# Routed tiles of a fused attention and expert layer: rows split to fp16 halves before they are turned, and turned by DMA instead of by TensorE

## The chip, the cores and the metric

The kernel runs on one core of a Trainium2 chip, as one launch. Its engines are TensorE (PE, with its weight loads PEld), VectorE (DVE), ScalarE (ACT), GpSimd (POOL) and SyncE (SP), which only issues DMAs here. The metric is the device time of one execution in microseconds, the median of several runs. Before the change it is 1236.01 us.

## What is computed

The input has 2 sequences of 2048 tokens of 256 numbers in fp32. The first half is a delta-rule attention block with a residual. The second half, which the change touches, is a mixture of experts:

```python
x = x + attn(layernorm(x))                        # q, k, v by projection and causal convolution, chunks of 64
h = layernorm(x)
scores = sigmoid(h @ centroids.T)                 # 8 experts
_, top_idx = top_k(sigmoid(h @ centroids.T + routing_bias), 2)
top_w = softmax(scores at top_idx)
shared = sum over 2 shared experts of gelu(h @ Wfc_sh.T) @ Wproj_sh.T      # 256 -> 1024 -> 256
routed = sum over the 2 chosen experts of top_w * (gelu(h @ Wfc_r.T) @ Wproj_r.T)
out = x + h + shared + routed
```

All of it is to come out at fp32 accuracy. The expert matmuls reach it with fp16 operands: a number is scaled and split into a high fp16 half and a low one (the rest), and a product is made of three passes: high by high, high by low, low by high.

## The kernel before, in words

**Work.** The attention runs first, in groups of 512 tokens. Beside it the first seven 256-row tiles already go through the two shared experts. From about 590 us on only expert work is left, in *units*, each one tile of 256 rows by one expert: 10 units of the five *early* tiles (two shared experts each), 36 *routed* tiles, 8 units of the four *final* tiles. A routed tile holds rows that chose one expert. The rows come from the table `x2n_d` in DRAM through an indirect DMA, and its result rows go back by another one, to `yt_d`. The first four routed tiles are of two half tiles with an expert each.

**A unit.** PE turns the tile (`turn`, line 1449): four transposes of 128 x 128 fp32 into a PSUM bank, so that the model dimension lies on the partitions. ACT makes the fp16 high half of it (`x_high_half`, 1155), DVE the low half (`x_low_half`, 1937); both lie in `xs`, one buffer for even and one for odd tiles. PE's `up` then does 4 x 12 matmuls of 256 columns, ACT the gelu and the high half of its result, DVE the low half (`low`, 1746), PE's `down` 48 more matmuls, and DVE scales the result to `yo` (`y_of`, 1973).

**Order.** `late_units` (236) writes one order for PE, ACT and DVE alike: step k does `up` of unit k+1, `turn` of unit k+2, `down` of unit k. Most of the routed steps are a hardware loop over pairs of tiles (`Fori`), the rest is straight code. The argument `looped` says how far the loop goes: for PE and ACT over all units up to tile 41, for DVE up to tile 33. The engines wait for each other through counting semaphores: `x_turned`, `x_high`, `x_low`, `up_done`, `h_low`, `y_out` and so on.

**Queues.** POOL issues the gathers and the scatters. Per tile i: wait until PE has turned tile i-2 (its buffer `xg` is then free), gather tile i by two DMAs of 128 rows, wait for `y` of tile i-4, scatter that by two DMAs. SP loads the expert weights piece by piece (`load_piece`, 691) into `wstage`, where ACT and DVE split them (`split_high`, `split_low`); the last two of the 32 pieces are needed before the first routed tile. It also stores the sums of the early tiles (`store_acc`), and, when all scatters have landed (line 784), loads `yt_d` for the closing sums.

Of the kernel before, what the change touches and what calls it, by code (L numbers as in the profile page):

```python
# [7 lines left out]
ALU = mybir.AluOpType  # L8
# [84 lines left out]
def pieces_of(k):  # L93

    return range(EP + sum(LOADS[:k]), EP + sum(LOADS[:k + 1]))

# [139 lines left out]
def late_units(eng, turn, up, down, between=None, spare=None, looped=L_TILES):  # L236

    units = [(early_tile(v), e) for v in range(EARLY) for e in range(N_SH)]  # L240
    units += [(routed_tile(i), 0) for i in range(L_TILES)]
    base = N_SH * EARLY

    def step(k):
        if k + 1 < len(units):
            up(*units[k + 1])
        if k + 2 < len(units) and units[k + 2][1] == 0:
            turn(units[k + 2][0])
        down(*units[k])
        if spare and k + 1 < len(LOADS):  # L250
# [69 lines left out]
def build(nc, x, w_proj, conv_w, g_col, w_o, cent, bias, w_ffn,  # L320
          ident, lvl_masks, eye2, head_sel, head_ones, block_tri, row_iota, tile_iota, pref, lane_iota, col_iota, tok_base, part_iota, out):
    ctx = ExitStack()
    with ctx:
# [50 lines left out]
        assert late <= 8192  # L374

# [170 lines left out]
        x_low = sem("x_low")  # L546
        up_done = sem("up_done")
# [68 lines left out]

        def x_there(t):

            if t.routed:
                return x_gathered[t.par], 16 * XB * (t.half - G_ROUTED // 2 - (G_ROUTED % 2) * (1 - t.par) + 1 if t.half is not None  # L620
                                                    else t.i // 2 + 1)
            return x_loaded[t.par], 16 * t.loaded()

# [18 lines left out]
        def _(sp):  # L642
# [26 lines left out]
            def load_base(t):  # L669
# [9 lines left out]
                sp.dma_start(bt[t.par], rows_of(base_d, t.rows)).then_inc(base_in[t.par], 16)  # L679

# [119 lines left out]
        def _(pool):  # L800
# [82 lines left out]
            def tile_looped(k, j):  # L883
                t, done = looped_tile(k, j), looped_tile(k, j - SCATTER_LAG)
                pool.wait_ge(x_turned, t.turn - 1)
# [30 lines left out]
            def load_final(q):  # L916

                t = routed_tile(R_TILES + q)
                pool.wait_ge(x_turned, t.turn - 1)
# [11 lines left out]
        def _(act):  # L931
# [223 lines left out]
            def x_high_half(t):  # L1155
                act.wait_ge(x_turned, t.turn + 1)
# [27 lines left out]
            late_units(act, x_high_half, unit_of, nothing, spare=split)  # L1184
# [3 lines left out]
        def _(pe):  # L1188
# [260 lines left out]
            def turn(t):  # L1449
                pe.wait_ge(*x_there(t))  # L1450
                if not isinstance(t.g, int) or t.turn:

                    pe.wait_ge(x_low, t.turn)
# [16 lines left out]
            def up(t, e):  # L1470
# [8 lines left out]
                pe.wait_ge(x_low, t.turn + 1)  # L1479
# [27 lines left out]
            late_units(pe, turn, up, down, between, spare)  # L1507
# [3 lines left out]
        def _(dve):  # L1511
# [425 lines left out]
            def x_low_half(t):  # L1937
                dve.wait_ge(x_high, t.turn + 1)
# [65 lines left out]
            late_units(dve, x_low_half, unit_of, y_of, between=between, spare=split, looped=R_TILES)  # L2004
# [67 lines left out]
```

## Time and profile before

| | us |
|---|---|
| runs | 1230.71, 1236.26, 1236.01; median 1236.01 |
| the profiled execution's own time | 1232.95 |
| its span | 1231.2 |
| PE busy | 1114.2 (90%) |
| DVE busy | 694.7 (56%) |
| ACT busy | 622.5 (51%) |
| POOL busy | 365.0 (30%) |
| up passes (line 1378), 3072 matmuls | 352.9 |
| down passes (line 1398), 3264 matmuls | 373.2 |

The span is the time from the first to the last instruction in the trace; the execution's own time has the start and the end of the launch with it. Busy time of PE counts the modelled pipeline, so what two groups of matmuls cost is best read from the distance between their starts. The last two rows of the table are the largest groups of instructions: together they are about 60% of the span. Idle time of an engine matters only where another engine waits for it.

### The profile page before, as it was taken

The numbers are of one execution on the slowest core, as the hardware profiler recorded it, in microseconds if no ns is written. First come the engines' busy times: TensorE is split into PE (matmuls) and PEld (weight loads), VectorE is DVE, ScalarE is ACT, GpSimd is POOL, SyncE is SP. The second block draws the span as 40 slices with busy tenths as digits, with TensorE's granted clock in tenths as the row PEclk, the third lists the DMA queues.
The fourth block names the chain that finished last, engine by engine and source line by source line (L and its number), as shares of the span: only waits on it lengthen the run. The fifth ranks groups of instructions, "written<-read, shape, count | busy, mean of one in ns | idle before, by whom it ended". The sixth has DMA issues, their size and how long they took to land.

```text
span 1231.2 us, 25608 instructions
## 1 busy us (share of the span) xinstructions
PE 1114.2 (90%) x9320; PEld 959.5 (78%) x9321; DVE 694.7 (56%) x1211; ACT 622.5 (51%) x1117; POOL 365.0 (30%) x320
## 2 busy tenths in 40 slices
PE   4596889999999998877988989999999999999996
PEld 1464768787878787766877878898999998999996
DVE  4667857676767675575689642333333333333377
ACT  4565556756565655355633643444444444444442
POOL 0415343424252425122011112334334334333100
PEclk9698879999999999998999989999999999999998
DMA  3202020202020102253222421111111111111456
GB/s 131 69 18 69 1 77 1 78 10 78 10 78 10 61 10 95 78 156 112 95 86 78 138 61 57 43 50 52 43 51 49 45 51 47 47 51 51 145 197 230
DMA packets 54088, 86.36 MB, mean 70 GB/s; under 512 B 6656, under 2 KB 39296, under 8 KB 53888
## 3 DMA queue, kind: packets, MB, share of 16 engines
q1 hardware_dynamic: 46336, 64.37, 16.2%
q0 software_dynamic: 7680, 20.98, 5.5%
q8 instruction: 52, 0.85, 0.3%
q14 instruction: 20, 0.16, 0.0%
HBM read 60.16 MB, written 25.17 MB: 69 GB/s over the span
## 4 chain that ended last, share of the span: by engine, by line
PE 65%; DVE 11%; issue 11%; ACT 6%; POOL 5%; DMA 2%; SPq 0%; DVEq 0%; ACTq 0%; POOLq 0%
PE ps L1398 25%; PE ps L1378 22%; PE ps L1232 4%; PE ps L1389 3%; PE ps L1222 2%; PE ps L1297 2%; POOL W L823 2%; PE ps L1456 2%; POOL W L842 2%; PE ps L1304 1%; ACT W L1071 1%; DVE late_room L1749 1%; PE ps L1358 1%; DVE W L1560 1%; DVE W L1652 1%
## 5 line engine op out<-in xcount | busy, mean ns | idle before, releaser
L1378 PE MATMUL ps<-late_room,W 128*128 128x256 f16 x3072 | 352.9, 273 | 28.5 <-DVE late_room L1749 22.6
L1398 PE MATMUL ps<-W,late_room 128*128 (+1 forms) x3264 | 373.2, 274 | 0.3 <-DVE late_room L1749 0.3
L1378 PEld LDWEIGHTS ps<-late_room,W 128*128 (+1 forms) x3072 | 298.6, 98 | 70.4 <-DVE late_room L1749 28.5
L1398 PEld LDWEIGHTS ps<-W,late_room 128*128 128x128 f16 x3264 | 321.7, 99 | 40.4 <-DVE late_room L1749 0.5
L1097 ACT ACTIVATE ps<-ps 128x512 f32<-128x512 f32 x272 | 158.6, 583 | 354.5 <-PE ps L1378 316.8
L1749 DVE SCALAR_TENSOR_TENSOR late_room<-ps,late_room 128x512 f16<-128x512 f32 x272 | 181.0, 687 | 233.4 <-ACT late_room L1102 233.4
L1102 ACT ACTIVATE late_room<-ps 128x512 f16<-128x512 f32 x272 | 155.7, 595 | 2.5
L1560 DVE SCALAR_TENSOR_TENSOR W<-W 128x512 f32<-128x512 f32 x144 | 109.1, 758 | 10.2 <-ACT W L959 6.8
L940 ACT COPY W<-ps 128x512 f32<-128x512 f32 x112 | 61.5, 589 | 86.7 <-PE ps L1297 70.4
L1232 PE MATMUL ps<-W 128*128 128x512 f16 x384 | 97.3, 399 | 7.1 <-DVE W L1575 3.8
L1997 DVE TENSOR_SCALAR late_room<-ps 128x512 f32<-128x512 f32 x36 | 24.9, 691 | 97.7 <-PE ps L1398 97.7
L1232 PEld LDWEIGHTS ps<-W 128*128 128x128 f16 x384 | 38.7, 103 | 49.1 <-issue 10.2
L1297 PE MATMUL ps<-W 128*128 128x128 f32 x320 | 50.3, 307 | 18.3 <-DVE W L1610 11.1
L1297 PEld LDWEIGHTS ps<-W 128*128 128x128 f32 x320 | 45.7, 217 | 23.7 <-DVE W L1610 14.4
L862 POOL DMA_INDIRECT late_room<-x2n_d,gath x52 | 51.4, 988 | 30.9 <-POOL gath L886 21.2
L873 POOL DMA_INDIRECT yt_d<-late_room,scat x52 | 51.1, 983 | 29.2 <-POOL scat L891 21.3
L1206 PE MATMUL ps<-idt,W 128*128 128x128 f32 x256 | 39.8, 302 | 18.7 <-ACT W L1082 12.8
L823 POOL TENSOR_TENSOR W<-W 128x512 f32<-128x512 f32 x40 | 47.2, 1214 | 24.7 <-ACT W L1021 24.7
L1610 DVE TENSOR_TENSOR W<-W,ps 128x512 f32<-128x512 f32 x40 | 27.4, 684 | 46.8 <-PE ps L1304 46.8
L1206 PEld LDWEIGHTS ps<-idt,W 128*128 128x128 f32 x256 | 32.1, 158 | 23.9 <-issue 12.9
L846 POOL TENSOR_TENSOR W<-W 128x4 f32<-128x4 f32 x8 | 9.0, 1120 | 139.4 <-DVE W L1537 139.4
L862 POOL DMA_INDIRECT late_room<-x2n_d,idx x20 | 19.5, 976 | 90.1 <-PE ps L1456 76.4
(188 smaller groups left out, 1372.1 us busy)
## 6 DMA issues: line engine op xcount, KB each, us to landing
wstage<-in_w_ffn SPq DMA_DIRECT2D x40, 512.0 KB, 3.8
W<-yt_d SPq DMA_DIRECT2D x16, 512.0 KB, 5.8
late_room<-in_x SPq DMA_DIRECT2D x8, 512.0 KB, 4.6
W<-in_x SPq DMA_DIRECT2D x8, 512.0 KB, 4.1
x2n_d<-W SPq DMA_DIRECT2D x8, 512.0 KB, 3.1
base_d<-W SPq DMA_DIRECT2D x8, 512.0 KB, 3.6
late_room<-base_d SPq DMA_DIRECT2D x16, 256.0 KB, 4.2
acc_d<-late_room SPq DMA_DIRECT2D x12, 256.0 KB, 2.2
```

The source lines that it names most:

```text
L823: pool.tensor_tensor(CT[:, s - 1], AT, masks[:, s].unsqueeze(1).to_broadcast([P, GT, P]), ALU.mult).then_inc(masked, 1)
L862: pool.indirect_dma_start(out=xg[t.par][:, c], out_offset=None, in_=x2n_d, in_offset=bass.IndirectOffsetOnAxis(ap=rows, axis=0)).then_inc( ...
L940: act.copy(dst, ring.bank(name)).then_inc(ring.empty(n, name)[0], 1)
L1097: act.activation(up_bank(n, c), up_bank(n, c), ACT.Gelu, scale=1.0 / (X_SCALE * W_SCALE)).then_inc(gelu_done, 1)
L1102: act.activation(hs[b][:, 0, 2 * c:2 * c + 2].rearrange("p f t -> p (f t)"), up_bank(n, c), ACT.Copy, scale=H_SCALE).then_inc(h_high, 1)
L1206: by_tile(ring, n, name, lambda to, k: pe.transpose(to, src[:, k, d * P:(d + 1) * P], idt[:]))
L1232: last = pe.matmul(to, wp[:, hw, d, m * P:(m + 1) * P], xnT[:, hx, d], start=(q == 0), stop=(q == len(parts) - 1))
L1297: by_tile(bk, n, f"Y{s}", lambda to, k: pe.matmul(to, CT[:, s - 1, k], X[b][:, k], start=True, stop=True))
L1378: last = pe.matmul(up_bank(n, c)[:, f * XT:(f + 1) * XT], weight(slot, d, hw, cols), x_halves[:, hx, d], start=(q == 0), stop=(q == len(pa ...
L1398: last = pe.matmul(down_bank(b)[:, c * D:(c + 1) * D], hs[b][:, hh, f, c * P:(c + 1) * P], weight(slot, DB + f // 4, hw, cols), start=(q = ...
L1560: dve.scalar_tensor_tensor(conv_at(m, b), pre[:, m, t:t + GRP], cw[:, m, t:t + 1], conv_at(m, b), ALU.mult, ALU.add).then_inc(conv_step, 1)
L1749: dve.scalar_tensor_tensor(lo, up_bank(n, c), H_SCALE, hi, ALU.mult, ALU.subtract).then_inc(h_low, 1)
```

## The change

For the 36 routed tiles the order of splitting and turning is swapped. ACT and DVE now split the gathered rows as they lie in SBUF, into `xh` (new, one buffer for each parity, 128 x 2 x 2 x 256 fp16), and SP turns both halves with two DMA transposes per tile, one for each group of 128 rows, straight into `xs`. PE has no transposes for routed tiles. The split of a tile stands one step earlier in the common order than the turn did: step k splits the rows of unit k+3. The buffer `xg` is free for the next gather when DVE has made the low half (`row_low`), not when PE has turned it. The early and final tiles are turned by PE as before. The loops of PE and ACT now end at tile 31, as DVE's does, and the remaining tiles are straight code.

```diff
+def by_dma(t):
+    return t.routed and not (isinstance(t.g, int) and t.i >= R_TILES)
...
 def late_units(...)
-        if k + 2 < len(units) and units[k + 2][1] == 0:
+        if k + 2 < len(units) and units[k + 2][1] == 0 and not by_dma(units[k + 2][0]):
             turn(units[k + 2][0])
+        if rows and k + 3 < len(units) and units[k + 3][0].routed and by_dma(units[k + 3][0]):
+            rows(units[k + 3][0])
         down(*units[k])
...
             up(looped_tile(k, j + 1), 0)
-            turn(looped_tile(k, j + 2))
+            if rows:
+                rows(looped_tile(k, j + 3))
             down(looped_tile(k, j), 0)
...
+        xh = [sb(f"xh{b}", [P, XB, 2, D], F16) for b in range(2)]
...
 SP:
+            def turn_rows(t):
+                if not isinstance(t.g, int):
+                    settled(sp, up_done, 4 * (t.unit() - 1))
+                else:
+                    sp.wait_ge(up_done, 4 * (t.unit() - (1 if t.i >= 2 else N_SH - t.i * (N_SH - 1))))
+                settled(sp, row_low, t.i + 1)
+                for c in range(XB):
+                    sp.dma_start_transpose(out=xs[t.par].rearrange("p q d t -> p (q d) t")[:, :, c * P:(c + 1) * P],
+                                           in_=xh[t.par][:, c].rearrange("p q d -> p (q d)")).then_inc(rows_turned[t.par], 16)
...
                 for e in range(N_SH):
+                    if e and v + 2 >= EARLY:
+                        turn_rows(routed_tile(v + 2 - EARLY))
                     load_before(N_SH * v + e)
...
+            for i in range(2, PEELED):
+                turn_rows(routed_tile(i))
             for v in range(2):
                 load_base(final_tile(v))
+            pairs = (R_TILES - 2 - PEELED) // 2
+            with sp.Fori(PEELED // 2, PEELED // 2 + pairs) as k:
+                for j in range(2):
+                    turn_rows(looped_tile(k, j))
+            for i in range(PEELED + 2 * pairs, R_TILES):
+                turn_rows(routed_tile(i))
...
 POOL, tile_looped (and alike in gather_static):
-                pool.wait_ge(x_turned, t.turn - 1)
+                pool.wait_ge(row_low, t.i - 1)
...
 ACT:
+            def row_high_half(t):
+                act.wait_ge(*x_there(t))
+                if not isinstance(t.g, int) or t.i >= 2:
+                    act.wait_ge(rows_turned[t.par], 16 * X_TURNS * of_parity(t))
+                act.activation(xh[t.par][:, :, 0], xg[t.par], ACT.Copy, scale=X_SCALE).then_inc(row_high, 1)
...
-            late_units(act, x_high_half, unit_of, nothing, spare=split)
+            late_units(act, x_high_half, unit_of, nothing, spare=split, looped=R_TILES - 2, rows=row_high_half)
...
 PE, up:
-                pe.wait_ge(x_low, t.turn + 1)
+                if by_dma(t):
+                    pe.wait_ge(*turned_rows(t))
+                else:
+                    pe.wait_ge(x_low, turns(t) + 1)
...
-            late_units(pe, turn, up, down, between, spare)
+            late_units(pe, turn, up, down, between, spare, looped=R_TILES - 2)
...
 DVE:
+            def row_low_half(t):
+                dve.wait_ge(row_high, t.i + 1)
+                dve.scalar_tensor_tensor(xh[t.par][:, :, 1], xg[t.par], X_SCALE, xh[t.par][:, :, 0],
+                                         ALU.mult, ALU.subtract).then_inc(row_low, 1)
```

How the instructions stand: first SP's queue around the last weight pieces, before. `wstage` is the landing place of the weights, `acc_d` the store of an early tile's sums, `base_d` the residual rows; the square brackets name the semaphores waited for.

```order
L685 DMA late_room<-x2n_d 128x2x256 [waits x_turned]
L698 DMA wstage<-in_w_ffn 128x1024 [waits rw_low] x4
L679 DMA late_room<-base_d 128x2x256 [waits y_out]
L689 DMA acc_d<-late_room 128x2x256 [waits y_out]
L698 DMA wstage<-in_w_ffn 128x1024 [waits rw_low] x4
L689 DMA acc_d<-late_room 128x2x256 [waits y_out] x2
L679 DMA late_room<-base_d 128x2x256 [waits y_out] x2
```

The same place now (`late_room<-xh` is a tile's rows turned into `xs`, which lies in `late_room`):

```order
L737 DMA wstage<-in_w_ffn 128x1024 [waits rw_low] x2
L717 DMA_TRANSPOSE late_room<-xh 128x4x128 [waits up_done,row_low]
L717 DMA_TRANSPOSE late_room<-xh 128x4x128
L737 DMA wstage<-in_w_ffn 128x1024 [waits rw_low] x2
L728 DMA acc_d<-late_room 128x2x256 [waits y_out]
L717 DMA_TRANSPOSE late_room<-xh 128x4x128 [waits up_done,row_low]
L717 DMA_TRANSPOSE late_room<-xh 128x4x128
L728 DMA acc_d<-late_room 128x2x256 [waits y_out]
L717 DMA_TRANSPOSE late_room<-xh 128x4x128 [waits up_done,row_low]
L717 DMA_TRANSPOSE late_room<-xh 128x4x128
```

The pair of tile 0 stands between the last four weight loads, that of tile 1 between the last two stores, and the others follow. Second, ACT in the loop of the routed tiles, the end of one tile's unit and the start of the next, before (1097 is the gelu, 1102 the high half of its result, 1158 the high half of the turned tile):

```order
L1097 ACTIVATE ps<-ps 128x512 [waits up_done]
L1102 ACTIVATE late_room<-ps 128x512 [waits gelu_done] x2
L1156 REGISTER_ALU
L1158 ACTIVATE late_room<-ps 128x512 [waits up_done,x_turned]
L1096 ISA
L1097 ACTIVATE ps<-ps 128x512 [waits up_done]
```

And now (1152 is the gelu, 1157 its high half, 1220 the high half of the gathered rows):

```order
L1152 ACTIVATE ps<-ps 128x512 [waits up_done]
L1157 ACTIVATE late_room<-ps 128x512 [waits gelu_done] x2
L1217 ISA
L1219 ISA [waits x_gathered1]
L1220 ACTIVATE xh<-late_room 128x2x256 [waits rows_turned1]
L1151 ISA
L1152 ACTIVATE ps<-ps 128x512 [waits up_done]
```

The instruction has kept its place behind the unit's last high halves, but belongs to a tile one further on; it waits for the gathered rows and for the transposes that last read its buffer, where it waited for PE's turn. DVE's list changes in the same way.

## Rows read from the trace of the kernel before

**Rows 1.** The page, parts 1 and 2: engines; busy tenths in 40 slices.

```profile
PE 1114.2 (90%) x9320; PEld 959.5 (78%) x9321; DVE 694.7 (56%) x1211; ACT 622.5 (51%) x1117; POOL 365.0 (30%) x320
...
PE   4596889999999998877988989999999999999996
...
DVE  4667857676767675575689642333333333333377
```

**Rows 2.** Windows: us, busy us (x instructions) by engine, granted clock, DMA share, GB/s.

```profile
900.00:1000.00 100.00, 100.00 (x918) 90.03 (x917) 36.34 (x55) 43.38 (x81) 38.97 (x55) 1.00 0.15 47
...
sum 300.00, PE 300.00 PEld 270.11 DVE 107.64 ACT 131.13 POOL 117.96; mean PE 100.00 PEld 90.04 DVE 35.88 ACT 43.71 POOL 39.32
```

**Rows 3.** Timeline, two beats: start, duration, engine, line, what, [idle before].

```profile
960.08 0.60 PE L1456 MATMUL ps<-idt,late_room 128*128 128x128 f32 x4
...
960.52 5.40 PE L1398 MATMUL ps<-W,late_room 128*128 x48
...
965.76 5.40 PE L1378 MATMUL ps<-late_room,W 128*128 128x256 f16 x48
...
969.12 0.97 POOL L873 DMA_INDIRECT yt_d<-late_room,scat  x1 [0.30 <-issue]
...
971.00 0.60 PE L1456 MATMUL ps<-idt,late_room 128*128 128x128 f32 x4
...
972.65 0.62 ACT L1158 ACTIVATE late_room<-ps 128x512 f16<-128x512 f32 x1
...
973.52 0.68 DVE L1940 SCALAR_TENSOR_TENSOR late_room<-ps,late_room 128x512 f16<-128x512 f32 x1
...
981.91 0.60 PE L1456 MATMUL ps<-idt,late_room 128*128 128x128 f32 x4
```

**Rows 4.** Line L1456, PE's transposes: count, ns min/median/max.

```profile
L1456 PE MATMUL ps<-idt,late_room x196: 272/273/301, 599.1 to 1200.6; 128*128 128x128 f32 x196
```

**Rows 5.** Timeline, the last early tile's steps to the first routed tile.

```profile
707.52 5.40 PE L1378 MATMUL ps<-late_room,W 128*128 128x256 f16 x48
...
709.58 1.46 SPq L698 DMA_DIRECT2D wstage<-in_w_ffn  x2
...
712.76 0.60 PE L1456 MATMUL ps<-idt,late_room 128*128 128x128 f32 x4
...
714.89 2.02 ACT L1137 ACTIVATE W<-wstage 128x1024 f16<-128x1024 f32 x2
...
719.25 2.35 DVE L1917 SCALAR_TENSOR_TENSOR W<-wstage,W 128x1024 f16<-128x1024 f32 x2
...
723.49 0.82 PE L1389 MATMUL ps<-late_room,W 128*128 128x128 f16 x6 [4.88 <-issue]
```

**Rows 6.** Groups by line, 700 to 1231 us: busy us, mean ns, idle before.

```profile
L1940 DVE SCALAR_TENSOR_TENSOR late_room<-ps,late_room 128x512 f16<-128x512 f32 x44 | 30.0, 682 | 0.0
...
L1158 ACT ACTIVATE late_room<-ps 128x512 f16<-128x512 f32 x44 | 27.1, 616 | 0.0
...
L1917 DVE SCALAR_TENSOR_TENSOR W<-wstage,W 128x1024 f16<-128x1024 f32 x5 | 5.9, 1218 | 0.0
...
L1137 ACT ACTIVATE W<-wstage 128x1024 f16<-128x1024 f32 x4 | 4.0, 1073 | 0.0
```

**Rows 7.** Waits of SP's queue, 590 to 1231 us: total, times, longest.

```profile
SPq L784 <- DMA yt_d<-late_room,dst: 404.6, 1, 404.6
```

**Rows 8.** The page, parts 3 and 6: queues; issues, KB each, us to landing.

```profile
q1 hardware_dynamic: 46336, 64.37, 16.2%
...
wstage<-in_w_ffn SPq DMA_DIRECT2D x40, 512.0 KB, 3.8
...
acc_d<-late_room SPq DMA_DIRECT2D x12, 256.0 KB, 2.2
...
late_room<-x2n_d POOLq DMA_DIRECT2D x16, 128.0 KB, 2.4
...
late_room<-x2n_d,gath POOLq DMA_INDIRECT x52, 2.8
```

More of the change, by code:

```diff
@@ L95, in pieces_of, with turns @@
     return range(EP + sum(LOADS[:k]), EP + sum(LOADS[:k + 1]))
+X_TURNS = XB
+TURNED = EARLY
+def by_dma(t):
+    return t.routed and not (isinstance(t.g, int) and t.i >= R_TILES)
+def turns(t):
+    return t.g - G_EARLY if t.g < G_ROUTED else t.g - G_EARLY - R_TILES
 class Ring:
@@ L233, in final_tile, with late_units @@
     return Tile(G_FINAL + v, REST_ROWS[EARLY + v])
-def late_units(eng, turn, up, down, between=None, spare=None, looped=L_TILES):
+def late_units(eng, turn, up, down, between=None, spare=None, looped=L_TILES, rows=None):
     units = [(early_tile(v), e) for v in range(EARLY) for e in range(N_SH)]
@@ L546, in build @@
         x_low = sem("x_low")
+        row_high = sem("row_high")
+        row_low = sem("row_low")
+        rows_turned = [sem(f"rows_turned{b}") for b in range(2)]
         up_done = sem("up_done")
@@ L615, in weight, with of_parity, turned_rows @@
             return W[:, bass.ds(slot + k, 1), half, cols].rearrange("p a n -> p (a n)")
+        def of_parity(t):
+            return t.half - G_ROUTED // 2 if t.half is not None else t.i // 2
         def x_there(t):
             if t.routed:
-                return x_gathered[t.par], 16 * XB * (t.half - G_ROUTED // 2 - (G_ROUTED % 2) * (1 - t.par) + 1 if t.half is not None
-                                                    else t.i // 2 + 1)
+                return x_gathered[t.par], 16 * XB * (of_parity(t) + 1)
             return x_loaded[t.par], 16 * t.loaded()
+        def turned_rows(t):
+            return rows_turned[t.par], 16 * X_TURNS * (of_parity(t) + 1)
         def conv_at(m, b):
@@ L867, in gather_static @@
                 t = routed_tile(i)
-                pool.wait_ge(x_turned, t.turn - 1)
+                if i >= 2:
+                    pool.wait_ge(row_low, i - 1)
+                else:
+                    pool.wait_ge(x_turned, EARLY - 1 + i)
                 for c in range(XB):
@@ L884, in tile_looped @@
                 t, done = looped_tile(k, j), looped_tile(k, j - SCATTER_LAG)
-                pool.wait_ge(x_turned, t.turn - 1)
+                pool.wait_ge(row_low, t.i - 1)
                 pool.tensor_copy(gath[:, j, :], idx[:, bass.ds(t.i * XB, XB)]).then_inc(gath_copied, 1)
@@ L918, in load_final @@
                 t = routed_tile(R_TILES + q)
-                pool.wait_ge(x_turned, t.turn - 1)
+                if q < 2:
+                    pool.wait_ge(row_low, R_TILES - 1 + q)
+                else:
+                    pool.wait_ge(x_turned, EARLY + q - 1)
                 for c in range(XB):
@@ L1155, in x_high_half @@
             def x_high_half(t):
-                act.wait_ge(x_turned, t.turn + 1)
+                act.wait_ge(x_turned, turns(t) + 1)
                 act.wait_ge(up_done, 4 * (t.unit() - (1 if t.routed else N_SH)))
@@ L1450, in turn @@
                 pe.wait_ge(*x_there(t))
-                if not isinstance(t.g, int) or t.turn:
-                    pe.wait_ge(x_low, t.turn)
+                if turns(t):
+                    pe.wait_ge(x_low, turns(t))
                 for d in range(DB):
@@ L1478, in up @@
                     pair_slots[t.i] = slots
-                pe.wait_ge(x_low, t.turn + 1)
+                if by_dma(t):
+                    pe.wait_ge(*turned_rows(t))
+                else:
+                    pe.wait_ge(x_low, turns(t) + 1)
                 for c in range(4):
@@ L1937, in x_low_half @@
             def x_low_half(t):
-                dve.wait_ge(x_high, t.turn + 1)
+                dve.wait_ge(x_high, turns(t) + 1)
                 hi, lo = (xs[t.par][:, q].rearrange("p d t -> p (d t)") for q in range(2))
                 dve.scalar_tensor_tensor(lo, turn_bank, X_SCALE, hi, ALU.mult, ALU.subtract).then_inc(x_low, 1)
+            def row_low_half(t):
+                dve.wait_ge(row_high, t.i + 1)
+                dve.scalar_tensor_tensor(xh[t.par][:, :, 1], xg[t.par], X_SCALE, xh[t.par][:, :, 0],
+                                         ALU.mult, ALU.subtract).then_inc(row_low, 1)
             def unit_of(t, e):
@@ L2002, in between @@
                     router(part)
-            late_units(dve, x_low_half, unit_of, y_of, between=between, spare=split, looped=R_TILES)
+            late_units(dve, x_low_half, unit_of, y_of, between=between, spare=split, looped=R_TILES - 2, rows=row_low_half)
 def constants():
```

## The prediction, made before the changed kernel was run

> **What bounds the kernel now.** I read the page's first two parts first, to see which engine is busy and in which part of the span [rows 1]: PE 90% over all, and 9 in every slice from the 25th to the last but one, where DVE stands at 3. Then the windows of the routed stretch [rows 2]: in 800 to 1100 us PE is busy 300.00 us out of 300, at a granted clock of 1.00 (full speed, the 2.4 GHz level), with DVE at 36%, ACT 44%, POOL 39% and the DMA engines at 0.15. So in this stretch every nanosecond of PE's own work is a nanosecond of the span, and what the other engines do is free as long as it comes in time.
>
> Then the timeline of one beat [rows 3]. The reader is to see the pattern: 4 transposes at 960.08, 48 down matmuls at 960.52, 48 up matmuls at 965.76, 4 transposes at 971.00. A beat is (981.91 - 960.08)/2 = 10.915 us for each routed tile. The transposes take 960.52 - 960.08 = 0.44 us of it (the 0.60 in the row counts the modelled tail of the last one; the start of the next group is what matters), the two matmul groups 5.24 us each: 10.48 us without the transposes, 0.435 us less. In that row pattern the up pass that ends at 971.00 is followed on ACT by the last high halves and the x high half (ends 973.27) and on DVE by the x low half (ends 974.20). All transposes of the kernel, 196, are in one group [rows 4]: 5 early tiles, 36 routed, 8 final, by 4.
>
> **What goes.** PE loses 36 x 4 = 144 transposes and their waits: 36 x 0.435 = 15.7 us. Most of the 36 stand in the full stretch. The first two are worth a look. Tile 0's turn (712.76) is followed by the down pass, DVE's y, two weight splits, and only then PE's restart at 723.49 [rows 5]: this chain hangs on the end of the down pass, so it moves forward by the whole 0.44. I count all 36.
>
> **What is exchanged.** ACT's high half (616 ns from PSUM) and DVE's low half (682 ns from PSUM) [rows 6] are replaced by the same arithmetic on the gathered rows in SBUF, also 128 x 512. The nearest rows are the weight splits from SBUF [rows 6]: 1073/2 = 0.54 us on ACT for 512 elements and 1218/2 = 0.61 us on DVE (two SBUF inputs, as here). So about 0.1 us less for each engine, and with strided halves perhaps 0.1 us more; hidden either way: ACT and DVE are busy 44 and 36 us in 100 [rows 2]. I take zero.
>
> **What is added.** Per tile two DMA transposes on SP, each turning 128 rows of 512 fp16 numbers (128 KB), four 128 x 128 blocks. SP stands still from the last store of the early tiles to 1145 us (its one wait is 404.6 us [rows 7]), so issuing costs nothing there. The time they have: rows of tile i are split behind the up pass of tile i-2, so the low half is ready about 3.2 us after that pass ends (974.20 - 971.00 [rows 3]). PE then does a down, an up and a down pass before it needs tile i: 3 x 5.24 = 15.7 us. That leaves 12.5 us for issue, both transposes and the semaphore. Two limits follow. One is latency: with two buffers, the beat is (3.2 + L + 5.24)/2, below 10.48 while L is below 12.5. The other is rate: a pair must take the queue less than D = 10.48 us.
>
> No transpose by DMA is in the trace, so D is bounded by other rows. Below: 256 KB out of SBUF land 2.2 us after issue, and the 128 KB rows of the final tiles 2.4 us [rows 8]; a pair at plain speed is 3 us. Towards the other end: SP's queue passed 46336 packets in 16.2% of 16 engines' span [rows 8], 0.162 x 1231.2 x 16 / 46336 = 0.069 us per packet on an engine. If a pair is cut into the 256-byte rows of its blocks, that is 2 x 128 x 4 = 1024 pieces, 64 per engine, 4.4 us. In 32-byte pieces it would be 512 per engine, 35 us, and in single 2-byte numbers 8192 per engine, 565 us. The nearest row is the plain transfer of equal size; I take D = 4 to 5 us, which is hidden with 7 us to spare, and keep the rest for the slower rival.
>
> The Trainium skill bears on this twice. *DMA: Bandwidth & Descriptors*, section "Latency and other measured facts", gives DMA transposes 261 GB/s in one kernel; an estimate by it is 1.0 us of moving per pair, less than the rows' lower bound. *VectorE: DVE Perf Modes*, section "The three transpose paths", speaks against the change: 1309 ns by DMA for one 128 x 128 block, 390 ns on TensorE. Eight blocks one after the other would be an estimated 10.5 us, just at the beat without transposes, so even this leaves the sum as it is but no reserve. On PE the trace disagrees with such single-shot figures (0.11 us for each of a run of four [rows 3]), so I give the 1309 ns little weight as a rate.
>
> **Waits added and what queues behind them.** ACT's row split waits for the gathered rows, and behind it stand the gelus of the next unit, for which PE waits. POOL's order per beat is gather, then the scatter of a tile four earlier, which waits for y [rows 3]. The scatter ahead of tile i's gather ends 970.09 - 965.76 = 4.3 us after the down pass that it waits for, and that pass ends 5.24 us behind the up pass of tile i-4: so the gather starts 9.6 us after the end of that up pass; it lands (2.8 us [rows 8]) some 15 us after that end. It is split behind the up pass of tile i-2, at 2 x 10.48 + 1.8 = 22.8 us. Nearly 8 us to spare. The first two gathers wait for turns of early tiles, as before, and are over a beat ahead of their splits. DVE's wait on ACT's half is the one it has now. PE's wait on x_low becomes a wait on the transposes. The split of the buffers xh waits for the transposes of two tiles earlier, over by then.
>
> **The last weight pieces.** SP's queue now has tile 0's pair ahead of the last two weight loads. The pair waits for the low half of tile 0, near 705.5; the loads wait for the splits until 709.58 [rows 5], so the pair's wait holds nothing. Their data does share the engines: if the pair takes over 4 us, the loads (3.8 us to landing [rows 8], ACT's split at 714.89) slip by the excess less about 1 us, and the first routed tile with them. At 4.4 us: nothing.
>
> **Sum.** 36 x 0.435 off, nothing added: -15.7 us. The profiled execution took 1232.95 us (span 1231.2), so 1217.3; the median shown is 1236.01, by which it would be 1220.3. I take 1219, between the two. The likeliest case's own range is 1212 to 1224 (the before runs alone differ by 5.5 us).
>
> **Rivals.**
> *The transposes set the beat (slower).* Place: SP's queue, tiles 2 to 35. From D = 10.48 us the beat is D; at 10.95 us the gain is eaten (34 x 0.46 = 15.7); beyond it each microsecond costs 34. At D = 12: 1219 + 34 x 1.52 = 1271; at 35 us, 1219 + 834 = 2053. For it: no such operation in the trace, small pieces are what a transpose must come down to somewhere, and the engines are shared with gathers and scatters. Against it: the DMA engines are 0.15 busy in the stretch [rows 2], and it needs more than three times a plain transfer's time. Chance 0.25, of which 0.03 for the far ends.
> *At the edge.* D or L close to the limits (D 10.6 to 11.3, or L about 13 since gathers and scatters interleave): 1230 to 1242, no measurable change. For and against as above. Chance 0.10.
> *A late start.* The first pair delays the last weight pieces, or the first splits wait for a gather: D = 8 us gives 8 - 4 = 4 us of slip less 1, so 1222. One-off, still faster. For it: [rows 5] has about a microsecond of slack there. Against it: D would have to be well above 4.4. Chance 0.12.
> *PE does not keep its rate.* The end of the PE loop moves from tile 41 to tile 31, ten tiles more are straight code. A straight pass takes 712.76 - 707.52 = 5.24 us [rows 5], a looped one the same [rows 3], so I give this 0.01 (about 1225).
> The forecast has the rest, 0.52.
>
> **How the numbers follow.** Faster or slower here means by more than 0.5%, 6 us, about what a measurement of this kernel can tell from no change. Faster: 0.52 + 0.12 + 0.01 = 0.65. Same: 0.10. Slower: 0.25. The range: 1211 below, with 0.02 under it; above, it takes in the late start, the edge and the mildest of the slower rival, up to 1246, with 0.18 beyond.
>
> **What would show it.** In the page after: 52 PE transposes in place of 196, and a beat of 10.48 us between starts of down passes at 900 to 1000 us, PE still 100.00 at clock 1.00. DMA_TRANSPOSE issues on SP, 72 of them, with a time to landing under 6 us. PE without a wait on DMA in the routed stretch. Wrong if up matmuls (now L1439) wait for the xs transposes by DMA: then the beat equals what the queue takes per pair. The late-start rival is seen at the first routed tile: PE starting it later than 723. If ACT's split idles on the gather, my count of POOL's order is off.

## The result, and the profile after

| | before | after |
|---|---|---|
| median of 6 runs each, us | 1231.94 (1229.38 to 1236.26) | 1223.01 (1220.9 to 1225.27) |
| the profiled execution's own time | 1232.95 | 1220.9 |
| its span | 1231.2 | 1218.9 |

The ratio is 0.9921, 95% interval 0.9896 to 0.9946: faster by 8.9 us in the medians and by 12.1 us between the two profiled executions, where 15.7 us had been forecast. The time lies in the range and the sign is right. The median of 1236.01 us given above for the kernel before is that of its first three runs; with three more it is 1231.94. The question is where the rest of the 15.7 us went.

The page of the changed kernel, parts 1 and 2, answers to [rows 1]. PE has 144 instructions and 13.8 us less, and its row of tenths looks as before:

```profile
PE 1100.4 (90%) x9176; PEld 945.5 (78%) x9177; DVE 694.4 (57%) x1211; ACT 623.2 (51%) x1117; POOL 366.6 (30%) x320
...
PE   4596979999999998886999989999999999999996
```

The window of 900 to 1000 us answers to [rows 2]:

```profile
900.00:1000.00 100.00, 100.00 (x919) 89.64 (x917) 38.92 (x59) 47.50 (x89) 42.15 (x58) 1.00 0.28 75
```

PE is still full at the full clock. The other engines do a little more per microsecond because the tiles follow each other faster. The DMA share rose from 0.15 to 0.28, and that is the transposes: it is 0.15 again in the run without them (no_transposes, below).

The timeline of two beats answers to [rows 3]:

```profile
954.44 5.40 PE L1459 MATMUL ps<-W,late_room 128*128 x48
...
956.09 0.64 ACT L1220 ACTIVATE xh<-late_room 128x512 f16<-128x512 f32 x1
...
956.97 0.68 DVE L2008 SCALAR_TENSOR_TENSOR xh<-late_room,xh 128x512 f16<-128x512 f32 x1
957.75 12.97 SPq L717 DMA_TRANSPOSE late_room<-xh  x4
...
959.68 5.40 PE L1439 MATMUL ps<-late_room,W 128*128 128x256 f16 x48
...
964.92 5.40 PE L1459 MATMUL ps<-W,late_room 128*128 x48
...
970.16 5.40 PE L1439 MATMUL ps<-late_room,W 128*128 128x256 f16 x48
```

Down, up, down, up, and no transposes between them. The beat is 964.92 - 954.44 = 10.48 us, as computed. The rows are split at 957.65, and PE wants them turned at 970.16, as many microseconds later (12.5) as the prediction had counted.

The issues of the DMA transposes on SP, by line (count, ns min/median/max):

```profile
L717 SPq DMA_TRANSPOSE late_room<-xh x72: 1189/1259/2379, 707.9 to 1095.2; - x72
```

One issue holds SP for 1.26 us, a pair for 2.5 us. A plain load is issued in 0.43 us (rows of the launch, below). Tile 0's pair alone took longer, 3.47 us.

The DMA queues of the changed kernel in 800 to 1080 us (packets, MB, share of 16 engines):

```profile
q0 software_dynamic: 5101, 13.90, 15.8%
q1 hardware_dynamic: 29920, 7.61, 13.1%
...
late_room<-xh SPq DMA_TRANSPOSE x54
```

29920 / 54 = 554 packets for each transpose is a little too many, since two plain loads of 256 KB are in this queue too; by the packets that 108 more transposes add in x3 (below), (87630 - 29920) / 108, it is 534. The time is 0.131 x 280 / 54 = 0.68 us of all 16 engines for one, and the 26.1 points by which x3's queue is busier give the same. Before, this queue carried nothing there.

What PE waited for in 740 to 1100 us, the whole list:

```profile
PE ps L1450 <- issue: 1.0, 2, 0.5
```

No wait on a DMA. ACT waited there for PE's up passes alone, never for a gather. The two gaps that are there begin the up passes of tiles 2 and 3, the first row below being tile 0's:

```profile
725.39 8.56 PE L1450 MATMUL ps<-late_room,W 128*128 128x128 f16 x96 [4.88 <-issue]
733.86 5.40 PE L1459 MATMUL ps<-W,late_room 128*128 128x256 f16 x48
739.09 8.10 PE L1450 MATMUL ps<-late_room,W 128*128 128x128 f16 x96
747.21 5.43 PE L1459 MATMUL ps<-W,late_room 128*128 x48
753.17 8.57 PE L1450 MATMUL ps<-late_room,W 128*128 128x128 f16 x96 [0.54 <-issue]
761.77 5.43 PE L1459 MATMUL ps<-W,late_room 128*128 x48
767.70 8.54 PE L1450 MATMUL ps<-late_room,W 128*128 128x128 f16 x96 [0.51 <-issue]
776.26 5.42 PE L1459 MATMUL ps<-W,late_room 128*128 x48
781.52 1.69 PE L1439 MATMUL ps<-late_room,W 128*128 128x256 f16 x14
```

### The profile page after: what moved, and what is told of

Read it like the earlier page. It is cut to its first block, busy times and chain, and to the rows that moved or that the text cites. A ratio compares the mean times of both kernels' runs of the same rounds, so it can differ in the third digit from the quotient of the medians.

```text
span 1218.9 us, 25333 instructions
## 1 busy us (share of the span) xinstructions
PE 1100.4 (90%) x9176; PEld 945.5 (78%) x9177; DVE 694.4 (57%) x1211; ACT 623.2 (51%) x1117; POOL 366.6 (30%) x320
## 4 chain that ended last, share of the span: by engine, by line
PE 65%; issue 11%; DVE 10%; ACT 7%; POOL 5%; DMA 2%; SPq 0%; DVEq 0%; ACTq 0%; POOLq 0%
PE ps L1459 25%; PE ps L1439 23%; PE ps L1293 3%; PE ps L1450 3%; PE ps L1283 2%; PE ps L1358 2%; POOL W L872 2%; POOL W L891 2%; PE ps L1365 1%; ACT W L1126 1%; PE ps L1419 1%; DVE W L1716 1%; DVE W L1624 1%; PE ps L1401 1%; ACT W L995 1%
## 5 line engine op out<-in xcount | busy, mean ns | idle before, releaser
L1012 ACT ACTIVATE W<-ps 128x512 f32<-128x512 f32 x48 | 28.5, 593 | 31.9 <-PE ps L1293 30.7
```

## The experiments

Twelve runs were made; of two, one_ahead and x5, the beat is what counts, and the table has the others. It cuts each profiled execution in three: up to ACT's first normalise of an x tile (the start of the work), from there to PE's last transposes of an early tile (the attention, with early tiles beside it), and from there to the end (the part that the change speeds up). All in us, of the profiled execution; "ratio" is to runs of the kernel before on the same chip.

| kernel | first x tile | up to the last early turn | from there to the end | median (runs), ratio [95%] |
|---|---|---|---|---|
| before | 10.59 | 680.78 | 539.83 | 1231.94 (6) |
| before_again | 10.82 | 678.15 | 540.03 | 1230.77 (1) |
| pe_only | 12.87 | 677.21 | 539.92 | 1231.77 (1) |
| loops_only | 12.62 | 684.92 | 540.06 | 1237.16 (12), 1.0025 [1.0001, 1.0048] |
| after | 12.92 | 680.80 | 525.18 | 1223.01 (6), 0.9921 [0.9896, 0.9946] |
| after_again | 12.60 | 685.24 | 526.76 | 1222.87 (7), 0.9917 [0.9886, 0.9948] |
| no_transposes | 12.85 | 685.04 | 525.51 | 1220.79 (7), 0.9916 [0.9887, 0.9945] |
| all_routed | 12.36 | 677.99 | 523.05 | 1217.92 (6), 0.9888 [0.9859, 0.9917] |
| all_routed_2 | 12.68 | 682.04 | 521.88 | 1213.91 (6), 0.9861 [0.9829, 0.9893] |
| compact | 10.94 | 677.92 | 522.04 | 1213.75 (6), 0.9862 [0.9824, 0.9900] |
| hoist | 12.54 | 683.34 | 528.22 | 1225.9 (1) |
| x3 | 12.43 | 682.84 | 527.13 | 1224.16 (1) |

**before_again** and **after_again**: the two kernels unchanged.

> The kernel before once more, for a second profile. The profile after the change has 12.3 us less span than that of before, against 15.7 forecast; 2.3 us of the gap lie between 599 and 691 us, where both kernels run the same instructions and the profile after shows a granted clock of 0.91 to 0.98 in place of 1.00. Theory A (the clock's dips in the attention and early-tile stretches differ from execution to execution, whatever the kernel): this second profile of the same kernel has its dips elsewhere or of another size, and the time from 0 to the turn of the last early tile (691.4 in the first profile) moves by 1 to 3 us, while the beat in the routed stretch stays 10.915 us to 0.01. Theory B (the dips at 610 to 690 belong to the changed kernel): this profile has a clock of 1.00 from 590 to 690 again, and the same 691.4 to 0.3 us.

> The changed kernel once more, with five rounds. Theory A (run-to-run clock dips in the shared stretch): the clock of 590 to 690 us differs from the 0.91 to 0.98 of its first profile, and the distance from the turn of the last early tile to the end of the last down pass is the same as before to 0.2 us. Theory B (dips belong to the change): the same dips at the same places. On the time: what I can add up of the first two profiles as the change's own is 0.45 (tile 0's turn) + 0.55 (pair tiles) + 13.4 (31 beats) = 14.4 us, so a ratio of 0.988; the first six runs said 0.9921. Inside 0.985 to 0.991 for the sum, at 0.993 if something outside the profiled part of the program costs 5 us.

Measured: the table. The ratio repeats, 0.9917, just above the 0.985 to 0.991 that had been added up. Neither theory A nor B came true as a whole. The last early turn of before_again is 2.4 us earlier than in the first profile, as A says, but its clock is 1.00 from 610 to 690 us, as B says; after_again shows the dips of its first profile again (0.91 at 610 to 630 and 650 to 690 us), as B says, but the time from the last early turn to the end, which should have stayed to 0.2 us, is 1.6 us longer (of which 1.07 us in the stretch of the pair tiles, see "Tiles 1 to 4's turns" below). Within one kernel runs spread over 11 us (1215.77 to 1227.1 for after_again), and the column in the middle shows where: 678 to 685 us for the same code. So one profiled execution tells the first column well, the last to 1.6 us, and the whole time badly.

**no_transposes** leaves the DMA transposes out; the routed tiles are computed from what lies in `xs`.

```diff
                 settled(sp, row_low, t.i + 1)
-                for c in range(XB):
-                    sp.dma_start_transpose(...).then_inc(rows_turned[t.par], 16)
+                sp.sem_inc(rows_turned[t.par], 16 * X_TURNS)
```

> The changed kernel with the 72 DMA transposes left out (SyncE only raises the semaphore, so the routed tiles are computed from whatever lies in xs; the result is not the reference's). Theory A (the transposes are wholly hidden): no difference to the changed kernel, ratio to before equal to its to 0.002, beat 10.48 us. Theory C (the transposes cost something that the beat doesn't show, by their load on the DMA engines or by the first weights coming late): 2 to 6 us faster than the changed kernel.

Measured: the ratio of after_again run beside it, 0.9916 to 0.9917, and 525.51 us in the last column against 525.18 and 526.76. All 72 transposes, their issue, their packets and their share of the engines cost no time that can be measured. The intervals of the two ratios reach 3.6 and 3.8 us to either side; the traces say more, with 437.75 us from tile 4's up pass to the end against 437.38 and 437.85 with the transposes.

**all_routed** turns the rows of the final tiles by DMA too, so that no PE transpose is left behind the early tiles.

```diff
 def by_dma(t):
-    return t.routed and not (isinstance(t.g, int) and t.i >= R_TILES)
+    return t.routed
```

(SP issues their pairs behind the routed ones and between the loads of the closing sums, and POOL's gathers for the final tiles wait for `row_low`.)

> The changed kernel with the eight units of the final tiles also split in row order and turned by DMA, so that only the five early tiles are turned by PE. In the final stretch a beat with PE's turn is 10.915 us and without it 10.48. If the transposes stay hidden beside the loads of the closing sums, 8 x 0.435 = 3.5 us less than the changed kernel, ratio to it 0.997. If they queue behind the 512 KB loads of the sums (6 us to landing each, five or more in a row), up passes of the final units wait and it is 2 to 10 us slower than the changed kernel. I expect the first for units 0 to 3 and some wait on units 4 or 5: net between 0 and -3.5 us.

Measured: 1217.92 against 1222.87 for after_again on the same chip, and 2.1 to 3.7 us less in the last column. PE has 32 instructions less (9144 against 9176), the eight final turns, and eight turns are 8 x 0.435 = 3.5 us. From tile 4's up pass to the end it takes 434.09 us (434.07 in all_routed_2) against 437.38 and 437.85 with PE's turns: 3.3 to 3.8 us less, so all eight came off and no pair of transposes waited behind the loads of the closing sums.

**loops_only** is the kernel before with the loops ending where the change ends them.

```diff
-            late_units(act, x_high_half, unit_of, nothing, spare=split)
+            late_units(act, x_high_half, unit_of, nothing, spare=split, looped=R_TILES - 2)
-            late_units(pe, turn, up, down, between, spare)
+            late_units(pe, turn, up, down, between, spare, looped=R_TILES - 2)
```

(DVE's from `R_TILES` to `R_TILES - 2`.)

> The kernel before with one part of the change alone: the loops of PE, ACT and DVE end at tile 31, the rest is straight code; all turning stays on PE. Theory A (only the turns matter): same as before, ratio 0.998 to 1.002, and the beat 10.915 us in both straight and looped tiles. Theory D (the longer PE program costs time in the shared stretch, where three of four profiles of kernels with it showed the last early tile's turn 3 to 7 us later than the two profiles of before): ratio 1.002 to 1.005, with clock dips between 610 and 690 us and the last early tile's turn after 692.

Measured: slower by 0.25% [0.01, 0.48], an interval that only just leaves out zero. The last column is untouched, 540.06 us: the additional straight tiles run at the rate of the loop. A cost that every trace shows is in the first column, at the launch. ACT's first instruction waits for the first weights; its row in before_again, loops_only and pe_only:

```profile
7.62 1.28 ACT L935 ACT_TABLE_LOAD   x1 [7.62 <-DMA W<-in_w_proj]
```

```profile
9.42 1.28 ACT L935 ACT_TABLE_LOAD   x1 [9.42 <-DMA W<-in_w_proj]
```

```profile
9.67 1.28 ACT L935 ACT_TABLE_LOAD   x1 [9.67 <-DMA W<-in_w_proj]
```

**pe_only** shortens PE's loop alone, ACT and DVE stay as before.

> The kernel before with PE's loop alone ending at tile 31, ACT's and DVE's loops left as they are. If the length of PE's straight code is what delays the launch: first x tile at 12.3 to 12.9 us, as in loops_only. If it is the length of the whole program, or ACT's and DVE's own code: between 10.7 and 12 us, or unchanged at 10.7.

Measured: first x tile at 12.87 us, as in the kernels with all three loops shortened. So it is PE's straight code, longer by ten tiles, that delays the launch. How is seen in SP's queue, first in before_again, then in pe_only:

```profile
3.17 0.43 SPq L660 DMA_DIRECT2D W<-in_lvl_masks  x1
3.65 0.43 SPq L660 DMA_DIRECT2D W<-in_eye  x1
4.12 0.44 SPq L660 DMA_DIRECT2D W<-in_head_ones  x1
4.60 0.45 SPq L660 DMA_DIRECT2D W<-in_w_o  x1
```

```profile
3.65 1.09 SPq L660 DMA_DIRECT2D W<-in_eye  x1
4.78 0.81 SPq L660 DMA_DIRECT2D W<-in_head_ones  x1
5.64 0.74 SPq L660 DMA_DIRECT2D W<-in_w_o  x1
```

From 3.65 us on three issues take about twice as long, and the first weights land 7.8 us after issue, where it was 5.6 and 5.8 in the two profiles of before:

```profile
W<-in_w_proj SPq DMA_DIRECT2D x1, 1024.0 KB, 7.8
```

The loads are the same, 1968 packets in the first 12 us, but from 3 to 6 us they move 0.83 MB in pe_only and 1.28 MB in before_again. Something shares their way. That it is the launch's own copying of PE's longer program is my reading; the profile has no record of it.

**hoist** loads the register addresses of the pair tiles' expert weights (tiles 1 to 3) earlier in PE's program, ahead of the down pass that stands before the tile's up pass (so by one pass, not by the two of the text below), to see whether PE's sequencer is what begins tiles 2 and 3 late.

```diff
-                if paired(t):
-                    pair_slots[t.i] = slots
...
+                if 1 <= later < PAIR_TILES:
+                    pair_slots[later] = [slot_of(routed_tile(later), c) for c in range(XB)]
```

> The changed kernel with the slot numbers of tiles 1 to 3 (half tiles with an expert each, whose weights are addressed through registers) loaded two passes earlier, ahead of a down pass instead of ahead of the up pass. The two gaps of 0.5 us before the up passes of tiles 2 and 3 are new with the change. Theory E (latency of the register loads right before the pass, which the transposes used to cover): the two gaps go, no others come, from the first routed tile's start to that of tile 4 is 1 us shorter (55.1 in place of 56.1). Theory F (PE's sequencer is the limit in these tiles, over 250 register operations on their weight addresses): the gaps move to before the down passes or into the passes, and the same distance stays at 56.1 to 0.3.

Measured: the gaps ahead of the up passes went, new ones came inside them (0.4 to 1.1 us, not shown) and where the loads now stand, and they are larger:

```profile
737.34 5.40 PE L1459 MATMUL ps<-W,late_room 128*128 128x256 f16 x48 [1.23 <-issue]
742.58 7.05 PE L1450 MATMUL ps<-late_room,W 128*128 128x128 f16 x96
751.02 5.43 PE L1459 MATMUL ps<-W,late_room 128*128 x48 [1.40 <-issue]
```

From the first pair tile's up pass to tile 4's it takes 59.02 us, where theory E had said 55.1 and theory F 56.1. The places of the gaps are those of theory F; its unchanged distance is not. No operand is late in these rows; further on one down pass waits 1.31 us for DVE's low half, behind an up pass that has gaps itself. So moving the loads moves the gaps, and that register instructions between the matmuls, not the matmuls, set the pace in these tiles is the likely reading; the profile has no record of PE's sequencer itself.

**one_ahead** splits the rows one step later, in the place where the turn stood.

```diff
             if rows:
-                rows(looped_tile(k, j + 3))
+                rows(looped_tile(k, j + 2))
```

> The changed kernel with the rows split one step later, where the turn stood, so that PE does one down pass and not three passes between the low half and the first use (the first pair of transposes issued behind the last weight loads). The beat is then 5.24 + 3.3 + L, with L from the low half to both transposes landed and PE released: it measures L. Theory A (L about 4 us: 2 x 1.25 us of issue on SyncE, then 1.5 us): beat 12.6 us, and 33 x (12.6 - 10.48) = 70 us more than the changed kernel, about 1292. Rival (L close to the 12.5 us that were free): beat near 20 us, about 1550.

Measured: 1333.97 us against 1292 expected, a beat of 972.81 - 959.50 = 13.31 us. The mean of twelve beats from 904.74 to 1068.63 us is 13.66, since in some an up pass takes 6.8 us in place of 5.4, at a granted clock of 0.97 over 900 to 1000 us. The timeline, and what PE waited for in 790 to 1100 us:

```profile
959.50 5.41 PE L1439 MATMUL ps<-late_room,W 128*128 128x256 f16 x48 [2.74 <-DMA late_room<-xh]
...
972.81 5.41 PE L1439 MATMUL ps<-late_room,W 128*128 128x256 f16 x48 [2.67 <-DMA late_room<-xh]
```

```profile
967.27 0.68 DVE L2008 SCALAR_TENSOR_TENSOR xh<-late_room,xh 128x512 f16<-128x512 f32 x1
968.05 2.50 SPq L717 DMA_TRANSPOSE late_room<-xh  x2
```

```profile
PE ps L1439 <- DMA late_room<-xh: 62.5, 23, 3.7
```

This measures the latency: the low half is ready at 967.95, PE starts at 972.81, 4.86 us later; 2.5 us of it are the two issues.

**x3** and **x5** issue each pair of tiles 2 to 35 three and five times, all but the first into a buffer that nobody reads. PE waits for all of a tile's pairs, and SP issues the additional ones when those of the tile before have landed.

```diff
+                for m in range(4):          # x3: range(2)
+                    for c in range(XB):
+                        sp.dma_start_transpose(out=spare_room[:, :, c * P:(c + 1) * P], in_=...)
```

> The changed kernel with every pair of transposes of tiles 2 to 35 issued five times, four of them into an unused buffer (PE waits for all ten; SyncE waits for the tile before to be done ahead of the four extra). Theory A (a transpose costs SyncE 1.25 us of issue and the queue little more): 12.5 us per tile and the wait, so the beat is 12.5 to 14 us and the time 1223 + 34 x (2 to 3.5) = 1290 to 1340. Rival (moving, not issuing, is the cost: the pair takes the queue 4.4 us or more): beat 22 us or more, over 1600.

> Each pair of DMA transposes of tiles 2 to 35 issued three times, twice into a buffer that nobody reads. SP's issue of six transposes is then about 7.5 us of the 10.48 us beat, and the pair that counts is first in the queue. Theory (the transposes hide as long as their queue time is below a beat; a pair costs 2.5 us to issue): beat still 10.48 us and time as after, about 1222 us. Rival (the queues' own work for a pair is more than its issue, so x5's beat of 13.5 us came from them): beat between 10.5 and 11 us or more.

Measured: x3's beat is 10.48 us and its time, 1224.16 us, is that of after's runs; x5's beats are 13.4 and 14.0 us and its time 1329.24 us. SP in x3, then SP, PE and PE's waits in x5:

```profile
951.63 5.16 SPq L726 DMA_TRANSPOSE wstage<-xh  x4
959.40 2.50 SPq L717 DMA_TRANSPOSE late_room<-xh  x2
962.12 5.15 SPq L726 DMA_TRANSPOSE wstage<-xh  x4
```

```profile
942.61 10.38 SPq L726 DMA_TRANSPOSE wstage<-xh  x8
953.34 2.50 SPq L717 DMA_TRANSPOSE late_room<-xh  x2
956.05 10.35 SPq L726 DMA_TRANSPOSE wstage<-xh  x8
```

```profile
954.51 7.08 PE L1448 MATMUL ps<-late_room,W 128*128 128x256 f16 x48 [3.31 <-DMA wstage<-xh]
...
967.88 5.41 PE L1448 MATMUL ps<-late_room,W 128*128 128x256 f16 x48 [1.05 <-DMA wstage<-xh]
```

```profile
PE ps L1448 <- DMA wstage<-xh: 53.9, 22, 4.2
```

Six transposes take 7.65 us of SP in a beat of 10.48 and are hidden, ten take 12.85 and are not. In x5 SP's pauses between its groups are 0.2 to 0.9 us, and five pairs in a beat of 13.7 us are 2.7 us each. So SP's issue is nearly all of a pair's rate: D is 2.5 us, 2.7 with the waits of x5. PE's up pass takes 7.08 us in every second beat of x5, at a granted clock of 0.93 over 900 to 1000 us. x3's last column is 1.95 us longer than that of the changed kernel's first profile. Nearly all of it is at the very end, where the last of the closing sums waits 2.03 us for its load from `yt_d` and not 0.27.

**compact** and **all_routed_2** ran side by side. compact is all_routed with the loops as long as before, which is possible because no tile in them differs any more; all_routed_2 is all_routed once more.

```diff
-            late_units(pe, turn, up, down, between, spare, looped=R_TILES - 2)
+            late_units(pe, turn, up, down, between, spare)
```

(ACT's loop likewise with `L_TILES - 2`, DVE's with `R_TILES`.)

> All 36 routed and 8 final units' rows turned by DMA, as in all_routed, but PE's and ACT's loops run to tile 41 and DVE's to 33, as in the kernel before; the straight code of PE is then about as long as before. Theory D (longer straight code costs about 1.9 us at the launch and some more in the stretch up to the first routed tile): the first x tile is normalised at about 10.7 us again instead of 12.4, and the time is 2 to 4 us below all_routed run beside it, near 1215 us, ratio about 0.986. Rival (the later start of the kernels with long code is chance, or comes from the DMA transposes' part of the program): start at 12.4 us again and the ratio of all_routed, 0.989.

> The kernel all_routed once more, beside compact on the same chip. Both theories: ratio near 0.989, first x tile at 12.4 us. The difference to compact is what is to be read: 2 to 4 us by theory D, under 1 us by its rival.

Measured: the launch came back, as the theory of the straight code says:

```profile
7.74 1.28 ACT L991 ACT_TABLE_LOAD   x1 [7.74 <-DMA W<-in_w_proj]
```

The first x tile is at 10.94 us, against 12.68 in all_routed_2. But the time of the runs did not follow: 1213.75 against 1213.91 us where 2 to 4 us had been expected. Six runs each, spread over 11 and 6 us, do not resolve the 1.7 us of the launch, and the "some more" that I had added to it has no support here; they do not rule it out either. Both kernels have ratios of 0.986 where the changed one has 0.9921 and 0.9917; what the traces show of that difference is the 3.3 to 3.8 us of the eight final turns.

## Why the prediction was right, point by point

**The bound and the beat.** Right. PE was full, the beat fell by 0.435 us, and DVE, ACT and POOL followed. From tile 4's up pass to PE's last group of 96 matmuls the kernel before takes 430.99 us (before_again) and the changed one 417.45: 13.54 us less, for 31 turns of 0.435, 13.5.

**Tile 0.** Right. From the last early turn to PE's restart it is 725.39 - 693.72 = 31.67 us, before 723.49 ([rows 5]) - 691.37 = 32.12: 0.45 us less.

**Tiles 1 to 4's turns: the step that was mis-sized.** I counted "all 36", though I had looked at the first only. The four turns that stood between the first pair tile's up pass and tile 4's should bring 1.74 us. That stretch took 56.72 us in before_again and takes 781.52 - 725.39 = 56.13: 0.59. The 1.05 us of gaps ahead of tiles 2 and 3 took nearly all the rest (before_again has one of 0.17 us there, the first profile of before none). The other profiles show that even the 0.59 is not certain:

| | first pair tile's up pass to tile 4's | from there to the end |
|---|---|---|
| before, before_again, pe_only, loops_only | 56.68, 56.72, 56.73, 56.72 | 451.03, 451.20, 451.08, 451.23 |
| after, after_again, no_transposes | 56.13, 57.20, 56.09 | 437.38, 437.85, 437.75 |
| all_routed, all_routed_2, compact | 57.28, 56.10, 56.14 | 434.09, 434.07, 434.23 |

So the four turns bring 0.6 us in some executions and cost 0.5 in others; in after_again and all_routed the gaps stand inside the up passes too and sum to 2.2 us. My reading: before, PE's sequencer had the time of the transposes to get through its register instructions; without them it is late. hoist supports it, since moving those instructions moved the gaps, but no run takes the instructions away. Together, for the first profile: 0.45 + 0.59 + 13.5 = 14.6 us, and the table's last column has 539.83 - 525.18 = 14.65.

**The loops' ends: the cost that I looked for in the wrong place.** The rival "PE does not keep its rate" had a chance of 0.01, and within the tiles that was right (540.06 us in the last column of loops_only). But the same edit delays the launch: 12.3 to 12.9 us against 10.6 to 10.9, so 1.4 to 2.3 us in every kernel with the longer PE code, and in none with the shorter. I had priced the straight code by its passes and not by its length. So the profiled execution gained 14.65 - 2.33 = 12.3 us of span, its middle column being equal.

**What stays open.** The medians moved by 8.9 and 9.4 us, 3 us less than that, and loops_only's 3.3 us (0.25% [0.01, 0.48]) is 1.3 more than its launch, which its interval, 0.1 to 5.9 us, does not set apart. The middle column varies by 8 us, with PE's clock in it: the window of 640 to 660 us of the changed kernel and of before_again reads

```profile
640.00:660.00 20.00, 17.29 (x157) 14.96 (x155) 18.14 (x23) 7.19 (x12) 2.90 (x1) 0.91 0.17 55
```

```profile
640.00:660.00 20.00, 16.48 (x164) 14.58 (x162) 18.14 (x26) 6.51 (x12) 0.00 (x0) 1.00 0.20 59
```

The granted clock, last column but two, is 0.91 there in nine of the eleven profiled executions with the longer code, all but pe_only and all_routed, and 1.00 in all three with the shorter. The middle column is 680.8 to 685.2 us in the nine and 677.2 to 680.8 in the five. The runs' times say something alike: loops_only has five at 1230.6 to 1232.3 us and seven at 1236.4 to 1239.9, the kernel before beside it thirteen at 1227.0 to 1233.5 and four at 1235.9 to 1237.4. That suggests that the longer PE code makes the slower stretch more frequent, but the kernel before has it too, and compact, with the shorter code, gained nothing over all_routed_2. I leave it open; it would take many profiled executions to count.

**Luck in the number.** The 1219 us was taken between 1217.3, from the profiled execution, and 1220.3, from a median of 1236.01 that six runs put at 1231.94. From 1231.94 the sum gives 1216.2, which misses the measured 1223.01 by 6.8 us where 1219 misses it by 4.0: a part of the nearness is luck in the base. The profiled execution missed by 3.6 us (1220.9 for 1217.3): 2.3 at the launch and 1.15 in the tiles 1 to 4.

**DVE and ACT.** The splits cost 0.68 and 0.64 us (x1 rows above), where 0.61 and 0.54 had been read from the weight splits: 0.07 and 0.1 more, within what was allowed, and hidden. Against the splits from PSUM that they replace (0.68 and 0.62) nothing was saved. Whether the strided halves are the reason is not shown.

**D and L.** D was taken as 4 to 5 us and is 2.5 (x3, x5), below the 3 us that I had given as the plain speed of a pair; L was allowed 12.5 us and is 4.9 (one_ahead). The pieces were guessed right, some 1070 packets per pair for the 1024 of 256 bytes, but not their price: 1.4 us for a pair on 16 engines, not 4.4. The 0.069 us for a packet came from a mix of larger ones, 64.37 MB / 46336 = 1.4 KB each ([rows 8]), against 7.61 MB / 29920 = 254 bytes here. The rivals "the transposes set the beat" and "at the edge" would have needed four times this D, or 2.6 times this L. The Trainium skill, *VectorE: DVE Perf Modes*, section "The three transpose paths", has 1309 ns for one 128 x 128 block by DMA; here one instruction turns 128 x 512, four blocks, and holds SP for 1259 ns. As a price for each block, which is how the prediction used it, the figure does not agree with this trace: the estimate of 10.5 us for a pair made from it was four times too long.

**The late start.** It did not happen. Tile 0's pair was issued at 707.92 and held SP for 3.47 us, and the last two weight loads followed at 711.92, 18.2 us behind the last early turn as before (709.58 - 691.37). ACT's waits in 600 to 740 us have

```profile
ACT W L1192 <- DMA wstage<-in_w_ffn: 0.2, 1, 0.2
```

at the last of these splits (718.55), where the kernel before had no wait: the pair took the slack and 0.2 us more from ACT. after_again has no such wait, and in neither did PE's restart move by it: 31.67 and 31.71 us behind the last early turn.

## What to carry to other kernels

Where one engine is busy 100 of 100 us, work taken off it is gained one to one, but only where its matmuls set the pace: look for stretches with "issue" gaps or register-addressed operands and count nothing there until they are read. An operation that no row shows can be bounded first by what stands still (here SP, and DMA engines at 0.15) and then measured by issuing it several times: x3 and x5 bracket it in two runs. And an edit that turns a loop into straight code has a price at the launch, seen only in the first 13 us of the trace.

## What the runs showed of the hardware

- A DMA transpose of 128 x 512 fp16 numbers from SBUF to SBUF: 1.19 to 1.26 us of issue in most cases (2.38 at most), 0.68 us of 16 engines, some 535 packets; two of them are there for PE 4.9 us after their input is ready.
- Ten more tiles of straight code in PE's program made ACT's first instruction, which waits for the first weights, later by 1.4 to 2.3 us (9.1 to 9.7 us against 7.4 to 7.7), with three of SP's issues at about twice their time meanwhile.
- Around matmuls whose weights are addressed by registers, PE shows gaps of 0.2 to 0.7 us once the four transposes between the passes are gone (after, after_again, all_routed), and of 1.2 to 1.4 us ahead of the down passes where those loads were moved (hoist).
